# A second wait in a unit's gathers: the seventh gather of a unit waits for the rows of its second to sixth

## The chip, the cores and the metric

The kernel runs on one core of one Trainium2 chip. The metric is the device time of one execution in microseconds (us). The kernel before takes 5981.97 us, the median of three runs (5981.73 to 5982.89).

## What is computed

A graph network with 12,500 nodes of 64 features and 200,000 edges, the edges sorted by their destination. Two graph attention layers with four heads, then one layer with an attention over edges for each feature:

```python
def _gat(x, src, dst, W, att_src, att_dst, bias, n):
    xw = (x @ W).reshape(n, H, D)
    a_src = jnp.einsum('nhc,hc->nh', xw, att_src)
    a_dst = jnp.einsum('nhc,hc->nh', xw, att_dst)
    logits = jax.nn.leaky_relu(a_src[src] + a_dst[dst], NEG_SLOPE)
    m = jax.ops.segment_max(logits, dst, num_segments=n)
    ex = jnp.exp(logits - m[dst])
    s = jax.ops.segment_sum(ex, dst, num_segments=n)
    alpha = ex / (s[dst] + EPS)
    out = jax.ops.segment_sum(xw[src] * alpha[..., None], dst, num_segments=n)
    return out.mean(axis=1) + bias
...
h   = relu(_gat(x, ..., W1, ...) + (x @ lW1 + lb1))
y   = _gat(h, ..., W2, ...) + (h @ lW2 + lb2)
x   = layernorm(x + y)
# last layer, for each edge: relu([x[src], x[dst]] @ W_lin.T + b_lin), softmax over the edges of a
# destination, weighted sum of [x[src], x[dst]], @ W_out.T + b_out
x   = layernorm(x + last(x))
```

## The kernel before

**Units and passes.** The 200,000 edges are cut into units of 1,536 edges, twelve chunks of 128. There are 131 units; the last has only three chunks. The kernel makes three passes over all units: p = 0 and p = 1 are the two attention layers (the attention passes), p = 2 is the last layer. In each pass the rows of the source nodes are gathered from a table in HBM into SBUF. A row of the attention passes is 72 floats (288 bytes) wide, 128 rows a gather; a row of the last pass is 128 floats. When a pass is over, the rows that it stored are the table of the next pass.

**The gathers.** GpSimd (POOL) does nothing in the passes but issue gathers: one indirect DMA for each chunk, twelve a unit, one after the other (line 1075). So there are 130 x 12 + 3 = 1,563 in a pass and 4,689 in all. They fill `rows`, a ring of RING = 6 units. Before a unit's first gather POOL waits until the unit's indices are staged (`idx_staged`) and until the sums of the unit that used this place of the ring are done (`sums_ready >= n - RING + 2` in the attention passes), and it adds one to `go`, a counter that nobody waits for. The first gather of a unit counts on a semaphore of its own, `first_in`, the other eleven on `rows_in`, 16 for each gather. The first three units of pass 0 gather raw rows of x before the table is made, the fourth unit waits for the table.

**Who uses the rows.** In the attention passes ACT's `strip_of` (lines 1700, 1704, 1707) waits until all twelve gathers of a unit have landed, copies their attention terms, then waits for the first gather of the next unit (`first_in`) and copies that. From the strip PE makes the transposes of `fronts`, DVE the running maxima (lines 1327, 1332), PE adds them up (2067), DVE makes the logits (1345 to 1357), ACT the exponential (1746), DVE the shares (1392), and PE the sums over the rows themselves (`sums_of`, line 2085), which raise `sums_ready`. ACT copies the sums (`keep_sums`, line 1752), and PE, DVE and ACT make the output row of the unit, which SP stores (line 987). In the last pass DVE reads the rows itself (lines 1569, 1577, 1590, 1641).

**Other transfers.** ACT's queue fetches `rel_t` for a unit ahead (line 854, 336 KB), SP's queue fetches `own` (967) and `cut` (956) and stores the rows (987). Each engine runs its own hand-written order of these steps; they meet in semaphores alone. The order of POOL and the one user of the rows that waits for them in the attention passes stand below.

Of the kernel before, what the change touches and what calls it, by code (L numbers as in the profile page):

```python
# [50 lines left out]
def build(nc, x, src, dst, W1, att_src1, att_dst1, b1, lW1, lb1, W2, att_src2, att_dst2, b2, lW2, lb2,  # L51
# [9 lines left out]
    G = 12  # L61
# [47 lines left out]
    def landed(p, c, each, tail, each3=None, tail3=None):  # L109


        before = p * (each * len(range(c.s, NU, RING)) - (each - tail if (NU - 1) % RING == c.s else 0))
        if p == 2 and each3 is not None:
            each, tail = each3, tail3
        return 16 * each * c.q + 16 * (before + (tail if c.at_least(NU - 1) else each))
# [5 lines left out]
    def rest_landed(p, c):  # L121

        return landed(p, c, G - 1, LASTC - 1, G - 2, LASTC - 2)

    def chunks(c):
        return LASTC if c.at_least(NU - 1) else G
# [6 lines left out]
    with ctx:  # L133
# [20 lines left out]
        def sem(name):  # L154
            return ctx.enter_context(nc.semaphore(name))
# [259 lines left out]
        rows_in = [sem(f"rows_in{s}") for s in range(RING)]  # L415
# [86 lines left out]
        go = sem("go")  # L502
# [35 lines left out]
        def units(eng, end=NU):  # L538
            for u in range(RING):
                yield Unit(u // RING, u % RING)  # L540
            with eng.Fori(1, (NU - RING) // RING) as q:
                for s in range(RING):
                    yield Unit(q, s)
            for u in range((NU - RING) // RING * RING, end):
                yield Unit(u // RING, u % RING)
# [498 lines left out]
        @block.gpsimd  # L1044
        def _(pool):
            nc.gpsimd.memset(ident[:, :], 0.0).then_inc(consts_ready, 1)
            nc.gpsimd.memset(ones[:, :], 1.0).then_inc(consts_ready, 1)
            nc.gpsimd.iota(col_i[:, :], [[1, W]], base=0, channel_multiplier=0).then_inc(consts_ready, 1)
            nc.gpsimd.iota(row_i[:, :], [[1, 1]], base=0, channel_multiplier=1).then_inc(consts_ready, 1)
            pool.wait_ge(consts_ready, 4)  # L1050
            nc.gpsimd.affine_select(out=ident[:, :], in_=ident[:, :], compare_op=ALU.not_equal, fill=1.0,
                                    base=0, pattern=[[-1, P]], channel_multiplier=1)\
                .then_inc(consts_ready, 1)
            nc.gpsimd.memset(rows_g[:, 0:G * RAW, D:D + 1], 1.0).then_inc(consts_ready, 1)
            pool.wait_ge(consts_ready, 6)

            for p in range(3):
                if p > 0:
                    pool.wait_ge(row_stored, 32 * NU * p)
                for c in units(pool):  # L1060
                    n = NU * p + c.u
                    raw = p == 0 and c.below(RAW)
                    pool.wait_ge(idx_staged, RAW if raw else n + 1)
                    if p == 0 and c.below(RAW + 1) and c.at_least(RAW):
                        for k in range(len(XLOADED)):
                            pool.wait_ge(x_moved[k], XSTORED[k])
                            pool.sem_inc(go, 1)
                    if not c.below(RING):
                        if p < 2:
                            pool.wait_ge(sums_ready, n - RING + 2)  # L1070
                        else:
                            pool.wait_ge(share_ready, 4 * (n - RING + 1))
                    pool.sem_inc(go, 1)
                    for j in range(chunks(c)):
                        nc.gpsimd.indirect_dma_start(rows_of[p][:, G * c.s + j, 0:D] if raw else rows_of[p][:, G * c.s + j, :],  # L1075
                                                     None, x if raw else halves[p],
                                                     bass.IndirectOffsetOnAxis(ap=idx_now[:, c.s, j:j + 1], axis=0))\
                            .then_inc(first_in[c.s] if j < (2 if p == 2 else 1) else rows_in[c.s], 16)
            pool.wait_ge(end_ready, 1)
            for k, u in enumerate((FULL - 1, FULL)):  # L1080
                n = 2 * NU + u
                pool.wait_ge(row_kept_v, n + 1)
                if k == 0:
                    pool.wait_ge(row_stored, 32 * n)
                else:
                    pool.wait_ge(tail_stored, 16)
                nc.gpsimd.indirect_dma_start(out, bass.IndirectOffsetOnAxis(ap=end_at[0:W, k:k + 1], axis=0),
                                             row_out[u % 2][:, :], None, bounds_check=N - 1, oob_is_err=False)\
                    .then_inc(tail_stored, 16)
            pool.wait_ge(row_stored, 32 * (NU * 3 - 2))  # L1090
            pool.wait_ge(tail_stored, 32)
            pool.wait_ge(flag_ready, 1)
            with pool.If(pool.value_load(flag[0:1, 0:1], min_val=0, max_val=1) > 0):
                general[1](pool)

        @block.vector
        def _(dve):
# [224 lines left out]
            def segment_most(p, n, c, parts):  # L1322


                dve.wait_ge(cut_in[c.k], cuts_loaded(p, c))
                for cuts, values, running, _ in parts:
                    done = nc.vector.tensor_tensor_scan(running, cuts[:, 0:-1], values, NEG, ALU.add, ALU.max)  # L1327
                done.then_inc(upto_ready, 1)
                dve.wait_ge(upto_ready, n + 1)
                for cuts, _, running, to in parts:  # L1330
                    span = running.shape[1]
                    done = nc.vector.tensor_tensor_scan(to[:, span - 1:HALO - 1:-1], cuts[:, span:HALO:-1],  # L1332
                                                        running[:, span - 1:HALO - 1:-1], NEG, ALU.add, ALU.max)
                done.then_inc(most_ready, 1)
# [908 lines left out]
```

## Time and profile before

| | |
|---|---|
| time, median of 3 runs | 5981.97 us |
| span of the profiled execution | 8154.7 us |
| instructions in it | 86920 |
| PE busy | 4073.2 us, 50% |
| DVE busy | 3734.1 us, 46% |
| ACT busy | 2927.8 us, 36% |
| POOL busy | 4442.8 us, 54% |
| DMA, mean over the span | 55 GB/s |

The profiled execution is far longer than an ordinary one, and no time of it other than its span is given. So a stretch of the profile can't be taken for a stretch of an ordinary execution unless one knows what the extra 2,173 us consist of. POOL's times are those of single gathers; "idle before" is the time since the end of the gather before, with what ended it behind the arrow. An idle time put down to "issue" is one in which the engine waited for nothing that the profile shows, "remote" is a semaphore whose last increment the profile doesn't show.

### The profile page before, as it was taken

Reading aid. Unit: us, or ns where it says so; the run is one execution under the profiler, and the core shown is the slowest. Engines: PE = TensorE matmul, PEld = TensorE weight load, DVE = VectorE, ACT = ScalarE, POOL = GpSimd, SP = SyncE. Lnnn points to the kernel's source line nnn. Section 1 sums busy time; section 2 is a strip of 40 time slices with the busy share of each in tenths; the row PEclk is TensorE's granted clock in tenths of the full one; section 3 lists DMA queues with packets and bytes.
Section 4 is the critical chain, followed back from the end, with each engine's and each line's share of the span. In section 5 each row is a group of like instructions: output and inputs, shape, how many; then the busy total and the mean of one; then the engine's idle time right before and its main releaser. Section 6 shows DMA issues by size and latency. Waiting matters only on the chain. (4 is left out here: it accounts for less than half of the span.)

```text
span 8154.7 us, 86920 instructions
## 1 busy us (share of the span) xinstructions
PE 4073.2 (50%) x21983; PEld 3747.4 (46%) x21983; DVE 3734.1 (46%) x9512; ACT 2927.8 (36%) x5694; POOL 4442.8 (54%) x4701
## 2 busy tenths in 40 slices
PE   4445445444553555555555553445544444455455
PEld 4444444444442444444444443444444444444445
DVE  3333333333343444444444443555555555555556
ACT  2222222222222444444444442334333333344344
POOL 4666666666655666666666645444444444444442
PEclk6555555555565555555555565555555555555555
DMA  5222222222212222222222221111111111111111
GB/s 117 56 51 54 52 51 53 52 51 52 53 46 48 55 54 54 56 55 54 54 56 55 54 55 52 56 54 54 56 54 54 53 53 53 53 53 55 54 54 37
DMA packets 354021, 444.78 MB, mean 55 GB/s; under 512 B 142024, under 2 KB 233574, under 8 KB 353360
## 3 DMA queue, kind: packets, MB, share of 16 engines
q0 software_dynamic: 150112, 217.86, 13.4%
q10 hardware_dynamic: 50400, 132.89, 4.7%
q1 hardware_dynamic: 153424, 93.06, 4.4%
q8 instruction: 35, 0.57, 0.0%
q14 instruction: 50, 0.41, 0.0%
HBM read 407.90 MB, written 39.55 MB: 55 GB/s over the span
## 5 line engine op out<-in xcount | busy, mean ns | idle before, releaser
L1075 POOL DMA_INDIRECT rows<-tab,idx_now x4653 | 4404.9, 947 | 3600.9 <-issue 1586.1
L2197 PE MATMUL psum<-hot,prob 128*128 128x112 f32 x3126 | 776.5, 406 | 889.3 <-issue 879.4
L2085 PE MATMUL psum<-share,rows 128*65 128x132 f32 (+10 forms) x6240 | 1175.4, 380 | 0.1
L2197 PEld LDWEIGHTS psum<-hot,prob 128*128 128x128 f32 x3126 | 708.3, 316 | 933.1 <-issue 928.1
L2085 PEld LDWEIGHTS psum<-share,rows 128*65 128x65 f32 x6240 | 1092.0, 223 | 5.8 <-DVE share L1392 0.2
L1382 DVE TENSOR_SCALAR share_prev<-psum,prev_all 128x4 f32<-128x4 f32 x258 | 57.2, 222 | 2262.8 <-remote 2255.0
L2181 PE MATMUL psum<-own,hot_t 112*128 112x64 f32 x3126 | 687.2, 416 | 763.6 <-DVE mix L1548 585.1
L2181 PEld LDWEIGHTS psum<-own,hot_t 112*128 112x128 f32 x3126 | 664.3, 325 | 795.5 <-issue 580.8
L1752 ACT ACTIVATE sums<-psum 65x448 f32<-65x448 f32 x260 | 140.6, 541 | 2068.1 <-remote 2053.4
L1590 DVE TENSOR_TENSOR near<-psum,rows 128x768 f32<-128x768 f32 x131 | 124.9, 953 | 1424.2 <-remote 1386.6
L1720 ACT ACTIVATE std<-mean_var,eps 112x1 f32<-112x1 f32 x262 | 77.7, 297 | 1868.4 <-DVE mean_var L1420 1756.1
L2112 PE MATMUL psum<-w_next,turned 65*112 65x72 f32 x262 | 83.6, 422 | 1084.6 <-ACT turned L1756 1084.5
L1685 ACT ACTIVATE hot_t<-away,ones 112x1536 bf16<-112x1536 f32 (+2 forms) x393 | 616.9, 1570 | 12.8
L1683 ACT ACTIVATE away<-rel_t,minus_row 112x1536 f32<-112x1536 bf16 (+1 forms) x393 | 612.9, 1560 | 13.0 <-DMA rel_t<-rel_runs 6.7
L2112 PEld LDWEIGHTS psum<-w_next,turned 65*112 65x112 f32 x262 | 58.1, 282 | 1118.7 <-ACT turned L1756 943.0
L1392 DVE TENSOR_TENSOR share<-hot,psum 128x400 f32<-128x400 f32 (+2 forms) x780 | 487.5, 681 | 2.0 <-issue 1.4
L1327 DVE TENSOR_TENSOR_SCAN psum<-cut,psum 48x224 f32<-48x224 bf16 (+3 forms) x524 | 448.3, 878 | 81.4 <-PE psum L2058 49.9
L2097 PE MATMUL psum<-w_heads,sums 65*112 65x65 f32 x2080 | 441.8, 390 | 1.5 <-DVE mix L1412 1.1
L2097 PEld LDWEIGHTS psum<-w_heads,sums 65*112 65x112 f32 x2080 | 414.0, 303 | 2.2 <-ACT sums L1752 2.1
L2115 PE MATMUL psum<-w_edge,turned 65*112 65x192 f32 x262 | 126.7, 586 | 560.4 <-ACT turned L1756 560.4
L1332 DVE TENSOR_TENSOR_SCAN most<-cut,psum 48x176 f32<-48x176 bf16 (+3 forms) x524 | 394.6, 774 | 13.9 <-DVE psum L1327 0.3
L1746 ACT ACTIVATE psum<-logit 128x48 f32<-128x48 f32 (+1 forms) x262 | 56.4, 215 | 955.0 <-issue 877.7
(246 smaller groups left out, 6228.3 us busy)
## 6 DMA issues: line engine op xcount, KB each, us to landing
rel_t<-rel_row ACTq DMA_DIRECT2D x256, 336.0 KB
rows<-tab,idx_now POOLq DMA_INDIRECT x4653
rel_t<-rel_runs ACTq DMA_DIRECT2D x128, 336.0 KB
own<-tab SPq DMA_DIRECT2D x262, 63.0 KB
cut<-cut_row SPq DMA_DIRECT2D x130, 120.2 KB
tab<-row SPq DMA_DIRECT2D x131, 112.0 KB
tab<-row SPq DMA_DIRECT2D x131, 63.0 KB
own<-tab SPq DMA_DIRECT2D x131, 56.0 KB
```

Of the source, the lines that this page charges most:

```text
L1075: nc.gpsimd.indirect_dma_start(rows_of[p][:, G * c.s + j, 0:D] if raw else rows_of[p][:, G * c.s + j, :], None, x if raw else halves[p], b ...
L1327: done = nc.vector.tensor_tensor_scan(running, cuts[:, 0:-1], values, NEG, ALU.add, ALU.max)
L1332: done = nc.vector.tensor_tensor_scan(to[:, span - 1:HALO - 1:-1], cuts[:, span:HALO:-1], running[:, span - 1:HALO - 1:-1], NEG, ALU.add, ...
L1392: nc.vector.tensor_tensor(to[:, j0:j1, :, 0:w], hot[c.k][:, j0:j1, 0:w].unsqueeze(2).to_broadcast([P, j1 - j0, H, w]), prob[c.k][:, j0:j1, ...
L1683: nc.scalar.activation(away[:, 0:e], rel_t[k][:, 0:e], ACT.Abs, bias=minus_row[0:W, 0:1]).then_inc(away_ready, 1)
L1685: nc.scalar.activation((hot_b if p < 2 else hot_t)[k][:, 0:e], away[:, 0:e], ACT.Relu, bias=ones[0:W, 0:1], scale=-1.0)\
L1752: nc.scalar.activation(sums_kept_in(c)[:, :, 0:w], summed[:, :, 0:w], ACT.Copy).then_inc(sums_kept, 1)
L2085: done = nc.tensor.matmul(summed[:, :, LO[j]:HI[j]], rows_g[:, at + j, 0:D + 1], of[:, j, :, 0:SUBS[j]], start=not opened, stop=j == chunk ...
L2097: done = nc.tensor.matmul(mixed_of(c)[:, h, :], sums_kept_in(c)[:, h, :], w_heads[p][:, h, :], start=True, stop=True)
L2112: nc.tensor.matmul(extra[:, 0:2 * H + D], turned[:, 0:W], w_next[:, :], start=True, stop=True)\
L2181: done = nc.tensor.matmul(added3[:, j, :], hot_t[k][:, P * j:P * j + P], own3[c.s][:, 0:D], start=True, stop=True)
L2197: done = nc.tensor.matmul(summed3, prob3[k][:, j, :], hot3[k][:, j, :], start=not opened, stop=j == chunks(c) - 1, skip_group_check=True)
```

## The change

Three lines are put into POOL's loop over the twelve gathers of a unit. In the attention passes POOL waits ahead of gather j = 6, the seventh, until `rows_in` of the unit's place has reached `rest_landed(p, c)` less 96. `rest_landed` is the count when all eleven gathers of the unit that raise `rows_in` have landed, so this is the count when five of them have: j = 1 to 5, the second to the sixth. Then it adds one to `go`. The last unit of a pass has three gathers and so no such wait. The third pass is as before.

```diff
@@ -1072,6 +1072,9 @@
                             pool.wait_ge(share_ready, 4 * (n - RING + 1))
                     pool.sem_inc(go, 1)
                     for j in range(chunks(c)):
+                        if p < 2 and j == G // 2:
+                            pool.wait_ge(rows_in[c.s], rest_landed(p, c) - 16 * (G // 2))
+                            pool.sem_inc(go, 1)
                         nc.gpsimd.indirect_dma_start(rows_of[p][:, G * c.s + j, 0:D] if raw else rows_of[p][:, G * c.s + j, :],
                                                      None, x if raw else halves[p],
                                                      bass.IndirectOffsetOnAxis(ap=idx_now[:, c.s, j:j + 1], axis=0))\
```

## Rows read from the trace of the kernel before

**Rows 1.** Groups by line, POOL: us 500 to 2400 (pass 0), us 5000 to 7800 (last pass)

```profile
L1075 POOL DMA_INDIRECT rows<-tab,idx_now x1264 | 1195.4, 946 | 706.9 <-issue 493.5 <-remote 213.4
...
L1075 POOL DMA_INDIRECT rows<-tab,idx_now x1351 | 1278.5, 946 | 1523.3 <-ACT idx_now L1673 1129.6 <-issue 393.7
```

**Rows 2.** Timeline of POOL at the start: first, twelfth, thirteenth gather (start, duration)

```profile
4.40 1.12 POOL L1075 DMA_INDIRECT rows<-in_x,idx_now  x1 [2.41 <-DVE idx_now L1105]
...
18.37 0.95 POOL L1075 DMA_INDIRECT rows<-in_x,idx_now  x1 [0.31 <-issue]
19.62 0.95 POOL L1075 DMA_INDIRECT rows<-in_x,idx_now  x1 [0.30 <-issue]
```

**Rows 3.** Timeline of all engines, one unit in the middle of pass 0

```profile
1402.29 0.54 ACT L1752 ACTIVATE sums<-psum 65x448 f32<-65x448 f32 x1 [10.11 <-remote]
...
1403.07 0.95 POOL L1075 DMA_INDIRECT rows<-tab,idx_now  x1 [3.33 <-remote]
1403.11 0.20 ACT L1707 ACTIVATE strip<-rows 128x4 f32<-128x4 f32 x1
...
1404.95 0.32 ACTq L854 DMA_DIRECT2D rel_t<-rel_row  x1
...
1407.09 4.70 PE L2085 MATMUL psum<-share,rows 128*65 128x52 f32 x24
```

**Rows 4.** Timeline of ACT and POOL, third and fourth unit of pass 0

```profile
166.23 0.54 ACT L1752 ACTIVATE sums<-psum 65x448 f32<-65x448 f32 x1 [2.57 <-PE psum L2085]
...
175.77 0.54 ACT L1752 ACTIVATE sums<-psum 65x448 f32<-65x448 f32 x1 [2.08 <-PE psum L2085]
...
176.55 0.95 POOL L1075 DMA_INDIRECT rows<-tab,idx_now  x1 [32.00 <-PE psum L2085]
```

**Rows 5.** Timeline of PE and DVE in the last pass

```profile
6012.47 0.35 PE L2197 MATMUL psum<-hot,prob 128*128 128x112 f32 x1 [2.54 <-issue]
...
6026.67 0.96 DVE L1590 TENSOR_TENSOR near<-psum,rows 128x768 f32<-128x768 f32 x1 [21.50 <-remote]
...
6041.17 0.96 DVE L1590 TENSOR_TENSOR near<-psum,rows 128x768 f32<-128x768 f32 x1 [0.61 <-PE psum L2204]
```

**Rows 6.** Waits of POOL over the whole span: us, times, longest

```profile
POOL rows L1075 <- DMA tab<-row: 96.9, 2, 52.3
POOL out L1087 <- DVE row_out L1426: 88.2, 2, 84.8
```

**Rows 7.** Timeline of POOL, first gather from the table in pass 0

```profile
97.41 0.94 POOL L1075 DMA_INDIRECT rows<-tab,idx_now  x1 [47.56 <-DMA tab<-x_tab]
```

**Rows 8.** Timeline of POOL and ACT at the start of pass 1

```profile
2475.28 0.94 POOL L1075 DMA_INDIRECT rows<-tab,idx_now  x1 [0.30 <-issue]
...
2476.53 0.95 POOL L1075 DMA_INDIRECT rows<-tab,idx_now  x1 [0.31 <-issue]
...
2477.85 0.25 ACT L1704 ACTIVATE strip<-rows 128x48 f32<-128x48 f32 x1 [7.21 <-DMA rows<-tab,idx_now]
...
2478.95 0.21 ACT L1707 ACTIVATE strip<-rows 128x4 f32<-128x4 f32 x1 [0.84 <-DMA rows<-tab,idx_now]
```

**Rows 9.** Timeline of SP's queue and POOL at the end of pass 0

```profile
2460.50 0.33 SPq L854 DMA_DIRECT2D rel_t<-rel_row  x1
...
2461.32 0.94 POOL L1075 DMA_INDIRECT rows<-tab,idx_now  x1 [44.55 <-DMA tab<-row]
```

**Rows 10.** Timeline of POOL and DVE at the start of the last pass

```profile
4873.30 0.95 POOL L1075 DMA_INDIRECT rows<-tab,idx_now  x1 [0.30 <-issue]
...
4880.52 0.31 DVE L1569 STREAM_TRANSPOSE outer<-rows 128x128 f32<-128x128 f32 x1 [10.35 <-DMA rows<-tab,idx_now]
```

**Rows 11.** The page's DMA queues: packets, MB, share of 16 engines' span

```profile
q0 software_dynamic: 150112, 217.86, 13.4%
q10 hardware_dynamic: 50400, 132.89, 4.7%
```

**Rows 12.** Groups by line, POOL, whole span

```profile
L1075 POOL DMA_INDIRECT rows<-tab,idx_now x4653 | 4404.9, 947 | 3600.9 <-issue 1586.1 <-ACT idx_now L1673 1248.4 <-remote 568.1
```

## The prediction

> **What bounds the kernel now.** The profiled execution took 8154.7 us of span and the runs have a median of 5981.97 us, so the first question is which of the profile's times an ordinary execution has too. I read the groups by line for POOL first. A gather is 0.95 us of work, in every pass [rows 1]. In pass 0 there are 1264 gathers in 1900 us, or 18.04 us for a unit of twelve; in the last pass 1351 in 2800 us, 24.87 us for a unit. Next the timeline of POOL where nothing holds it, at the start: the first gather starts at 4.40, the twelfth at 18.37 and the thirteenth, which belongs to the next unit and has a wait and an increment of `go` ahead of it, at 19.62 [rows 2]. So the pace is 1.25 us from start to start (0.95 of work and 0.30 between), a unit takes 12 x 1.25 = 15.0 us, and a wait that is already met costs nothing that shows.
>
> Then the timeline of a unit in mid-pass. POOL waits 3.3 us at the unit's first gather, and ACT has waited 10.1 us for the same thing, the sums of a unit [rows 3]. It looks as if the compute engines bound the passes. But in this unit PE's sums start at 1407.09 and are through 4.70 us later, 9.5 us after ACT's start at 1402.29 [rows 3], and where nothing is late ACT's next start follows them: 9.54 us for a unit (166.23 to 175.77) [rows 4]; in the last pass it takes 14.50 us (6026.67 to 6041.17), after a stretch in which PE's matmuls came one by one, 2.5 us apart, for nothing that the trace shows, and DVE waited 21.5 us [rows 5]. The late semaphores are PE's slow stretches, and I take them for the cost of being profiled. Without them compute needs 9.5 us a unit in the attention passes and 14.5 in the last, both less than POOL's 15.0.
>
> The median bears this out. 4,689 gathers x 1.25 = 5861 us. The start adds 4.4 [rows 2] and 47.3 for the table (47.56 less the usual 0.30) [rows 7], which makes 5913. On top come POOL's wait for the ring in pass 0, 32.0 [rows 4], the two turns between passes, 96.9, and the end, 84.8 [rows 6]: all of them would make 6127. These last four are too long in the profile, because there POOL is up to six units ahead when its gathers end, and would be one or two units ahead otherwise. 5982 lies between 5913 and 6127. So in an ordinary execution POOL issues gathers back to back through all three passes, and that sets the time.
>
> **The change, part by part.** It removes nothing and moves no transfer past another. It adds a wait and an increment of `go` ahead of the seventh gather of each of the 130 full units of passes 0 and 1, 260 in all. Behind the wait on POOL stand the unit's six other gathers and every later unit; for them wait ACT's `strip_of` and all compute behind it. SP's and ACT's own transfers have no part in the wait.
>
> What the sixth gather needs to land: of the gather that starts at 2475.28, ACT uses the rows at 2477.85, 2.57 us after its start; of the next, started at 2476.53, at 2478.95, 2.42 us [rows 8]. In both cases ACT was idle and waiting, so its start shows the landing. I take 2.50.
>
> What POOL needs to go on: at 175.77 ACT starts on the sums of unit 1, and POOL, idle for 32 us and waiting for the same increment, starts its gather at 176.55, 0.78 later [rows 4]. In mid-pass it is 0.78 again (1402.29 to 1403.07) [rows 3]. After a transfer, where SP and POOL both wait for the last store of the pass, SP issues at 2460.50 and POOL starts at 2461.32, 0.82 later [rows 9]. The instructions after the wait are the same there as here: an increment of `go`, then a gather. I take 0.78.
>
> So the seventh gather starts 2.50 + 0.78 = 3.28 us after the sixth instead of 1.25: 2.03 us more for a unit, 17.03 in place of 15.0. The wait is not in the cover of anything, since compute is done with its 9.54 us and waits for rows. A unit's compute just starts 2.03 us later.
>
> Where it is covered: the first three units of pass 0 are gathered before the 47.56 us wait for the table [rows 7], and the next three before the 32.0 us wait for the ring [rows 4]; 3 x 2.03 = 6.1 us goes under in each. If that cover is thinner, the six units cost up to 12 us. That leaves 254 units x 2.03 = 516 us. The turns between passes and the end stay as they are: the seventh gather's delay is over before the last gather of a pass. 5982 + 516 = **6498 us**, forecast 6500.
>
> The Trainium skill, "DMA: Bandwidth & Descriptors", "Anatomy of one DMA — SWDGE (gpsimd) path", gives a GpSimd DMA about 2.0 us fixed and bytes / 436e3 on top, so an estimated 2.08 us for 36.9 KB. Counted from the gather's start that is shorter than the 2.42 to 2.57 of [rows 8] and would make 1.61 us a unit and 6391 us; counted from the end of its 0.95 us of work it would make 2.56 us a unit and 6632 us. The rows lie between the two readings.
>
> **Bounds of the unknown.** The wait in mid-unit itself has no row. Least: POOL goes on as fast as ACT does after a landing; then 2.50 - 1.25 = 1.25 us a unit, 5982 + 318 = 6300. Most: the sixth gather lands late because other transfers are in its way. ACT's queue fetches `rel_t` 1.84 us after the strip's last copy (1403.11 to 1404.95) [rows 3]. In an ordinary execution that copy comes 2.42 us after the unit's first gather, so the fetch starts near 4.3, and the sixth gather at 6.25. The packets of one such fetch take 4.7% x 8154.7 / 387 = 1.0 us of all 16 DMA engines, those of one gather 13.4% x 8154.7 / 4689 = 0.23 us [rows 11]. If the whole fetch ran ahead of the sixth gather each time, the unit would lose 3.03 us: 5982 + 770 = 6750. A gather at the crowded start of the last pass needed 7.22 us (4873.30 to 4880.52) [rows 10], but there the table's, the edges' and the cuts' first loads of a pass are all out at once; I hold that for a few units at the start at most, some 10 us in all. Since the fetch is mostly over when the sixth gather's packets run, the value is nearest to the undisturbed 2.50.
>
> **The rivals.**
>
> *The landing is late in every unit* (3.03 us, 6750). For it: the timing above puts the fetch just ahead of the sixth gather. Against it: one microsecond of packets has two to be gone in. The Trainium skill, same page, "Queues, rings and completion order", says that each DMA engine takes turns between its queues packet by packet; by that a gather is delayed by at most what the other queue has left, and no run before shows a gather beside just one fetch.
>
> *POOL goes on sooner* (1.25 to 1.6 us, 6300 to 6390). For it: profiling may lengthen both terms. Against it: 0.78 to 0.82 three times.
>
> *The wait is swallowed* (not slower, 5982). The mechanism is the wait for `sums_ready` at the unit's first gather. If compute and not POOL bounded the attention passes, POOL would have slack there and the wait in mid-unit would only move it: 12 x 1.25 + 2.03 = 17.03 us against the profile's own 18.04 us [rows 1, 3]. It decides from a compute cycle of 17.03 us on. Against it: 9.54 us undisturbed [rows 4], and a cycle of 17 in two passes and 15 in the last would make 131 x 49 = 6419 us before, not 5982.
>
> *It gets faster*: only by shorter gathers, if spacing them kept the descriptor queue from filling. The 4,653 gathers from the tables take 4404.9 us, 0.947 each, where single ones in mid-pass take 0.94 to 0.95 [rows 12]: less than 15 us in all is there to be won.
>
> **How the numbers follow.** Forecast (2.0 to 2.2 us a unit, 6480 to 6545, with differences of profiled and ordinary runs 6400 to 6660): 0.78. Late landing, above 6660: 0.08. Sooner, below 6400: 0.07. Swallowed: 0.05. Faster: 0.02. A range of 6390 to 6670 leaves out somewhat less than 2 in 10. A measurement tells 0.2% (12 us) from nothing, and every case but the last two is far beyond it: slower 0.93, same 0.05, faster 0.02.
>
> **What the changed profile would show.** The sum is made for an ordinary execution. In the profiled one the wait is the rival's case: 17.03 is below 18.04, so its span should stay near 8155 us (within 1%), the first gather's idle time in mid-pass should shrink from 3.3 to about 1.3, and the seventh's should be 0.30 + 2.03 = 2.3 instead of 0.30, released by the gather's DMA. The seventh gather should start 3.3 us after the sixth. The last pass should be as it was. If the median rises by about 516 us while the span of the profile stays, the reading of the two kinds of execution was right. It is wrong if the seventh's idle time differs from 2.3, or if the median stays where it is, since POOL then didn't bound the attention passes.

## The result and the profile after

The changed kernel takes 6621.09 us, the median of four runs (6612.66 to 6623.88), against 5981.85 us for the kernel before (four runs, 5981.19 to 5982.89). The ratio is 1.1069, 95% interval 1.1056 to 1.1082: slower by 639 us. The forecast was 6500 us with a range of 6390 to 6670.

One thing has to be said before any number below can be read. The kernel before is not equally fast on all chips: where the results above were measured it takes 5982 us, on the chip of the second set of experiments 5989, but on those of the first and the third set 8185 and 8086, profiled or not. The first profile of the kernel before, with its span of 8154.7, is of the second kind, and so it is compared with the runs on such chips only. I call the two kinds quick and slow chips, though each was met at one time only, so that it is the chip and nothing else of that time isn't shown.

The page of the changed kernel comes from a quick chip; its span is its run's time, 6621.49 us, less 2 us:

```profile
span 6619.7 us, 87256 instructions
...
PE 3930.2 (59%) x21983; PEld 3609.8 (55%) x21983; DVE 3695.7 (56%) x9512; ACT 2961.8 (45%) x5694; POOL 4437.0 (67%) x4701
...
L1078 POOL DMA_INDIRECT rows<-tab,idx_now x4653 | 4390.6, 944 | 2105.6 <-issue 1564.2
...
L2200 PE MATMUL psum<-hot,prob 128*128 128x112 f32 x3126 | 669.4, 408 | 10.9 <-DVE prob L1644 10.9
...
rows<-tab,idx_now POOLq DMA_INDIRECT x4653, 2.5
```

The last line is of the page's DMA issues: 2.5 us from a gather's issue to its landing, the median of 4,653. The gathers' own work is as before, 0.944 us each [rows 12]. The timeline of all engines in mid-pass 0: the sixth gather of a unit, the seventh and the eighth, and ACT and DVE at a unit's sums:

```profile
1409.07 0.94 POOL L1078 DMA_INDIRECT rows<-tab,idx_now  x1 [0.30 <-issue]
...
1412.33 0.94 POOL L1078 DMA_INDIRECT rows<-tab,idx_now  x1 [2.32 <-DMA rows<-tab,idx_now]
...
1413.43 0.54 ACT L1755 ACTIVATE sums<-psum 65x448 f32<-65x448 f32 x1 [1.44 <-PE psum L2088]
1413.54 0.22 DVE L1385 TENSOR_SCALAR share_prev<-psum,prev_all 128x4 f32<-128x4 f32 x1 [2.06 <-PE psum L2088]
...
1413.58 0.94 POOL L1078 DMA_INDIRECT rows<-tab,idx_now  x1 [0.30 <-issue]
```

The seventh starts 3.26 us after the sixth, having idled for 2.32 us until the gathers' DMA released it. ACT waits 1.4 us for the sums that it waited 10.1 us for in the first profile [rows 3]. What ACT waits long for is now the rows themselves, as `strip_of` shows in the same timeline:

```profile
1404.05 0.21 ACT L1703 ACTIVATE strip<-rows 128x4 f32<-128x4 f32 x1 [7.88 <-DMA rows<-tab,idx_now]
...
1405.33 0.21 ACT L1710 ACTIVATE strip<-rows 128x4 f32<-128x4 f32 x1 [0.93 <-DMA rows<-tab,idx_now]
```

The page has it for all units of both attention passes, 5.7 us of waiting for the gathers in each:

```profile
L1703 ACT ACTIVATE strip<-rows 128x4 f32<-128x4 f32 x260 | 53.3, 205 | 1476.8 <-DMA rows<-tab,idx_now 1476.7
```

So compute stands behind POOL. In the last pass POOL waits for nothing. The groups by line of POOL, us 5000 to 6500; the idle time is the 0.30 us between gathers and no more:

```profile
L1078 POOL DMA_INDIRECT rows<-tab,idx_now x1203 | 1135.2, 944 | 366.6 <-issue 366.6
```

Compare [rows 1]: there the same pass had 1130 us of waiting in 2800. Its 1,563 gathers now take from 4625.85 to 6575.83 us, 1.25 us each.

**Where the 639 us are.** I read the start of every gather from POOL's timeline. In pass 0 the seventh gathers start 3.95 us after the sixth in the mean, with a median of 3.41; in pass 1 3.63 and 3.29. Against the plain 1.25 us the 260 gaps add 351.5 + 308.7 = 660.2 us. The first three of pass 0 account for 23.1 of it. They come ahead of the first gather from the table, and if the wait for the table covers them, 637.1 us are exposed. The measured difference is 639.2.

Most gaps are the forecast's 3.28, but not all. Every fourth unit, the same units in both passes (u = 13, 17, ... 129, and u = 9 as well in pass 1), has a gap of about 4.6 in pass 0 and 4.5 in pass 1. One pair of gathers of such a unit, from the timeline:

```profile
1042.06 0.94 POOL L1078 DMA_INDIRECT rows<-tab,idx_now  x1 [0.30 <-issue]
...
1046.81 0.94 POOL L1078 DMA_INDIRECT rows<-tab,idx_now  x1 [3.81 <-issue]
```

Sorted by u modulo 4, the medians are 3.39, 4.63, 3.40 and 3.38 in pass 0 and 3.27, 4.52, 3.27 and 3.27 in pass 1.

**Which part of the gap is longer.** The trace also holds each increment of `rows_in` by a gather that lands. So a gap can be cut in two at the last increment that the wait asked for: what the sixth gather needs to land, and what POOL needs from there to the seventh. The medians from the eleventh unit on:

| units of the changed kernel | sixth gather's start to the last landing | last landing to the seventh's start |
|---|---|---|
| pass 0, u not 1 modulo 4 | 2.59 us | 0.80 us |
| pass 0, u = 1 modulo 4 | 2.60 us | 2.02 us |
| pass 1, u not 1 modulo 4 | 2.47 us | 0.80 us |
| pass 1, u = 1 modulo 4 | 2.49 us | 2.02 us |

The rows are not late in the outliers. POOL goes on late: 2.02 us after the landing in 61 units (30 in pass 0, 31 in pass 1), 0.79 to 0.81 us in the 199 others, with nothing in between. The row above says so too. Its idle time is put down to "issue", since no semaphore was raised just ahead of it, where a plain gap has "DMA". POOL's waits over the whole span:

```profile
POOL rows L1078 <- issue: 1574.0, 4487, 4.9
POOL rows L1078 <- DMA rows<-tab,idx_now: 490.7, 196, 10.8
```

The 61 late ones are what the second line lacks of the 257 waits for gathers from the table. Together they cost 61 x 1.22 = 75 us.

The landing is what is long at the crowded start of pass 0, where the sixth and seventh unit have gaps of 11.70 and 8.55 us, 10.91 and 7.75 of it until the landing. The DMA engines are busy for 67% of the first 165 us there, and for 25% from us 1000 to 1165:

```profile
133.16 0.94 POOL L1078 DMA_INDIRECT rows<-tab,idx_now  x1 [10.76 <-DMA rows<-tab,idx_now]
...
155.43 0.94 POOL L1078 DMA_INDIRECT rows<-tab,idx_now  x1 [7.60 <-DMA rows<-tab,idx_now]
```

### The profile page after: what moved, and what is told of

It is laid out like the page before. It is cut to its first block and busy times, and to the rows that moved or that the text cites. A ratio compares the mean times of both kernels' runs of the same rounds, so it can differ in the third digit from the quotient of the medians.

```text
span 6619.7 us, 87256 instructions
## 1 busy us (share of the span) xinstructions
PE 3930.2 (59%) x21983; PEld 3609.8 (55%) x21983; DVE 3695.7 (56%) x9512; ACT 2961.8 (45%) x5694; POOL 4437.0 (67%) x4701
## 5 line engine op out<-in xcount | busy, mean ns | idle before, releaser
L2061 PE MATMUL psum<-ident,strip 128*48 128x128 f32 (+1 forms) x786 | 210.3, 405 | 1703.8 <-ACT strip L1710 1703.5
L2061 PEld LDWEIGHTS psum<-ident,strip 128*48 128x48 f32 (+1 forms) x786 | 83.1, 133 | 1789.2 <-issue 1776.0
L2184 PE MATMUL psum<-own,hot_t 112*128 112x64 f32 x3126 | 654.9, 403 | 319.7 <-DVE mix L1551 300.5
L2184 PEld LDWEIGHTS psum<-own,hot_t 112*128 112x128 f32 x3126 | 633.1, 312 | 345.3 <-issue 238.3
L1703 ACT ACTIVATE strip<-rows 128x4 f32<-128x4 f32 x260 | 53.3, 205 | 1476.8 <-DMA rows<-tab,idx_now 1476.7
L2200 PE MATMUL psum<-hot,prob 128*128 128x112 f32 x3126 | 669.4, 408 | 10.9 <-DVE prob L1644 10.9
L2200 PEld LDWEIGHTS psum<-hot,prob 128*128 128x128 f32 x3126 | 649.8, 319 | 11.1 <-DVE prob L1644 11.1
L2106 PE MATMUL psum<-ident,row 112*64 112x112 f32 x262 | 80.7, 308 | 270.6 <-DVE row L1429 266.3
```

Source lines behind the costliest of these rows:

```text
L2184: done = nc.tensor.matmul(added3[:, j, :], hot_t[k][:, P * j:P * j + P], own3[c.s][:, 0:D], start=True, stop=True)
L2200: done = nc.tensor.matmul(summed3, prob3[k][:, j, :], hot3[k][:, j, :], start=not opened, stop=j == chunks(c) - 1, skip_group_check=True)
```

## The experiments

Theory A: POOL's issue of gathers sets the time of an ordinary execution; a wait costs what its releaser is late, 2.50 us for the landing and 0.78 for going on, less the 1.25 that the next gather would have taken anyway. Rivals: the wait or its increment costs something in itself; compute takes the delay up; and, for the surplus over 3.28, ACT's fetch of `rel_t` delays the landings. The expectations below take the gathers of every fourth unit for late, which the table above does not bear out.

**First set, a slow chip (before: 8184.53 us, median of 13 runs).**

*The kernel before, profiled again.* No edit.

> The kernel before, unchanged, for a second profile. The profile of before had a span of 8154.7 us against a median of 5982; the profile of the changed kernel has 6619.7 against 6621. Theory 1, that profiling slows PE in this kernel whenever the gathers run ahead of it: the span is again near 8155, with 3.3 us of idle time ahead of each unit's first gather in passes 0 and 1. Theory 2, that the first profile caught a peculiar execution: the span is within 1% of 5982, the gathers run at 1.25 us from start to start through all passes, and the waits ahead of first gathers are gone but for the turns between passes.

Measured 8188.28 us, and the span is 8186.4. The span and the waits are those of theory 1, but its reason is wrong. The median of thirteen runs of the kernel before is 8184.53 us on this chip, so it is no odd execution; and on the quick chip the changed kernel's profiled run took what its other runs took, so it is no cost of profiling. POOL's waits in it:

```profile
POOL rows L1075 <- issue: 1605.4, 4449, 3.7
POOL rows L1075 <- ACT idx_now L1673: 1261.6, 65, 20.6
POOL rows L1075 <- remote: 586.1, 169, 3.7
```

They are those of the first profile within 4% [rows 12].

*The wait asks for the first gather only.*

```diff
-                            pool.wait_ge(rows_in[c.s], rest_landed(p, c) - 16 * (G // 2))
+                            pool.wait_ge(first_in[c.s], first_landed(p, c))
```

> The wait stays ahead of the seventh gather of the 260 units but asks only for the unit's first gather, which started 7.5 us before and lands 2.5 us after its start. Theory POOL pace (the wait costs what its releaser is late, nothing in itself): 5982 us within 0.2%. Rival (the wait and the increment of go in mid-unit cost POOL something themselves, for instance 0.8 us each time for going on): 260 x 0.78 = +203, 6185 us.

Measured 8195.84 us, ratio 1.0017 (1.0007 to 1.0028): +11 us. Two seventh gathers near the start of pass 0 (u = 6 and 7) come 7.67 and 4.98 us after the sixth, since the first gather landed that late; they are 10 of the 11 us. But for three more units at the start of pass 0 or 1 (1.44 to 2.67 us) the gap is 1.25 to 1.29 in the rest of both passes. So a wait that is met at once adds nothing to the gap. POOL has slack on this chip, so the time alone would not have shown it; the gaps do.

*The third gather waits for the first.*

```diff
-                        if p < 2 and j == G // 2:
-                            pool.wait_ge(rows_in[c.s], rest_landed(p, c) - 16 * (G // 2))
+                        if p < 2 and j == 2:
+                            pool.wait_ge(first_in[c.s], first_landed(p, c))
```

> The wait stands ahead of the third gather and asks for the unit's first. The first lands 2.50 us after its start, POOL goes on 0.78 us later, so the third gather starts 3.28 us after the first instead of 2.50: +0.78 us a unit. Theory POOL pace with landing 2.50 and restart 0.78: 254 to 260 units x 0.78 = +198 to +203, 6180 to 6185 us. Rival (restart is as quick as ACT's): 5982 us. Rival (a wait costs a full round trip wherever it stands, as 2.46 us a unit did in the change): 6620 us. If other transfers made the change's landings late, the surplus over 6185 is small here, since ACT's fetch of rel_t starts only 4.4 us after the unit's first gather.

Measured 8245.96 us, ratio 1.0073 (1.0056 to 1.0089): +61 us. The gap from the second to the third gather has a median of 1.98 us in pass 0 and 1.97 in pass 1. The first gather starts 1.25 us ahead of the second, so the third starts 3.22 us after the first: the chain of landing and going on is 3.2 us here too, and 0.72 us of it are exposed in the unit (the forecast said 0.78). Of 260 x 0.72 = 187 us the time shows 61.

*The fourth gather waits for the second and third.*

```diff
-                        if p < 2 and j == G // 2:
-                            pool.wait_ge(rows_in[c.s], rest_landed(p, c) - 16 * (G // 2))
+                        if p < 2 and j == 3:
+                            pool.wait_ge(rows_in[c.s], rest_landed(p, c) - 16 * 9)
```

> The wait stands ahead of the fourth gather and asks for the second and third. The third starts 2.5 us into the unit and lands at 5.0; ACT's fetch of rel_t is issued 4.4 us into it, so its packets are still ahead. Theory collision (what the change cost over 3.28 us a gap comes from ACT's fetch running just ahead of the sixth gather): gaps of 3.28 without the outliers of 4.6, 254 to 260 x 2.03 = +516 to +528, 6498 to 6510 us. Rival (the surplus has nothing to do with the fetch, such as gathers landing late every fourth unit by themselves): the same as the change, 6621 us, with a gap of 4.6 in every fourth unit.

Measured 8365.53 us, ratio 1.0218 (1.0201 to 1.0235): +181 us. The median gap is 3.60 us in pass 0 and 3.25 in pass 1, but the units fall into two sorts on this chip: in pass 0 every other unit both waits some 4 us at its first gather and has a gap of 4.1 to 4.3. Neither number of the expectation is met, since both were worked out for a quick chip. Yet the run is evidence on the fetch. In the units with the long gap ACT issues the fetch 1.9 us into the unit, just ahead of the third gather, for which the wait asks:

```profile
1420.32 0.95 POOL L1078 DMA_INDIRECT rows<-tab,idx_now  x1 [2.91 <-remote]
...
1422.19 0.32 ACTq L854 DMA_DIRECT2D rel_t<-rel_row  x1
...
1422.82 0.94 POOL L1078 DMA_INDIRECT rows<-tab,idx_now  x1 [0.30 <-issue]
...
1426.76 0.94 POOL L1078 DMA_INDIRECT rows<-tab,idx_now  x1 [3.00 <-DMA rows<-tab,idx_now]
```

From the twelfth unit of pass 0 on, 56 units have a gap above 3.9 us, and each has the fetch at that place; their third gather lands 3.39 us after its start, and POOL goes on after 0.80. In the 58 units with a gap under 3.5 no fetch is issued. So the third gather lands 0.9 us late where a fetch is issued just ahead of it.

**Second set, a quick chip (before: 5988.75 us, median of 7 runs).**

*The tenth gather waits for the second to ninth.*

```diff
-                        if p < 2 and j == G // 2:
-                            pool.wait_ge(rows_in[c.s], rest_landed(p, c) - 16 * (G // 2))
+                        if p < 2 and j == 9:
+                            pool.wait_ge(rows_in[c.s], rest_landed(p, c) - 16 * 3)
```

> The wait stands ahead of the tenth gather and asks for the second to ninth. The ninth starts 10 us into the unit, well after ACT's fetch of rel_t (4.4 us) and after SP's store, own and cut transfers (6.8 to 9.1 us into it, or up to 2 us earlier). Theory collision with rel_t: gaps of 3.28 without outliers, 6498 to 6510 us. Rival (gathers land late every fourth unit by themselves): 6621 us. Rival (SP's transfers, which now lie just ahead, delay it): gaps above 3.28 in most units, up to 6650 us.

Measured 6518.5 us, ratio 1.0887 (1.0869 to 1.0905): +530 us. POOL's waits:

```profile
POOL rows L1078 <- issue: 1348.8, 4425, 0.3
POOL rows L1078 <- DMA rows<-tab,idx_now: 610.5, 257, 11.2
```

The gap has a median of 3.26 us in pass 0, 3.28 in pass 1, with no outlier in pass 1 (3.19 to 3.95) and those of the start alone in pass 0. This is theory A to the number: 3.28 us a gap. The gaps add 551.5 us, 19.7 of them ahead of the first gather from the table: 531.8 exposed, 529.75 measured. The same wait three gathers later is 109 us cheaper than the change. What is missing are the outliers of every fourth unit, some of the late landings at the start, and the 0.13 us by which pass 0's median was above pass 1's. POOL goes on 0.80 us after the landing in all 260 units here, u = 1 modulo 4 among them.

*One address for the fetch, in the changed kernel.*

```diff
-            eng.dma_start(rel_t[c.k][:, 0:e], (rel_row if p < 2 else rel_runs)[bass.ds(UE * c.u, e)].partition_broadcast(W))\
+            eng.dma_start(rel_t[c.k][:, 0:e], (rel_row[0:e] if p < 2 else rel_runs[bass.ds(UE * c.u, e)]).partition_broadcast(W))\
```

> The change, and in the attention passes every fetch of rel_t reads the same 3 KB of HBM, unit 0's; leaves out: the destinations' places of the other units. In the change the seventh gather comes 4.6 instead of 3.3 us after the sixth in every fourth unit, the same units in both passes (9, 13, 17, ...). Theory address (the fetch of a unit whose 3,072 bytes lie badly in HBM takes longer, and 4 x 3,072 is a multiple of 4,096): the outliers are gone or stand in all units; gone makes 6621 less 2 x 30 x 1.25 = 6546 us. Rival (the period of four comes from elsewhere, from a queue or from time): 6621 us, outliers as they are.

Measured 6620.89 us, ratio 1.1055 (1.1037 to 1.1074). The outliers stand in the same units, 4.61 and 4.52 us in the median. The address is not their cause, and POOL's 2.02 us after the landing is as it was.

*A short fetch, in the changed kernel.* ACT's fetches write 16 of 112 partitions.

```diff
-            eng.dma_start(rel_t[c.k][:, 0:e], (rel_row if p < 2 else rel_runs)[bass.ds(UE * c.u, e)].partition_broadcast(W))\
+            eng.dma_start(rel_t[c.k][0:(W if eng is nc.sync or p == 2 else 16), 0:e], (rel_row if p < 2 else rel_runs)[bass.ds(UE * c.u, e)].partition_broadcast(W if eng is nc.sync or p == 2 else 16))\
```

> The change, and in the attention passes ACT's fetches of rel_t write 16 of the 112 partitions (48 KB instead of 336 KB); leaves out: the other 96 partitions, which keep older values. Theory collision (the fetch's packets make the sixth gather late): all gaps near 3.28, 254 to 260 x 2.03, 6498 to 6510 us. Rival (the surplus isn't the fetch's): 6621 us with the outliers of 4.6 in every fourth unit.

Measured 6614.18 us, ratio 1.1045 (1.1027 to 1.1064). A seventh of the fetch's bytes saves 7 us, and the gap of u = 57 in pass 0 is there as before, 4.68 us:

```profile
1039.61 0.95 POOL L1078 DMA_INDIRECT rows<-tab,idx_now  x1 [0.30 <-issue]
...
1044.29 0.94 POOL L1078 DMA_INDIRECT rows<-tab,idx_now  x1 [3.73 <-issue]
```

So ACT's fetch does not make the outliers. It does make gathers land late, but others than the one on which the seventh waits. In the changed kernel it is issued 4.3 us into the unit, as the prediction had it, 0.6 us after the fourth gather starts. From its own start the fourth gather then needs 3.67 us to land and the fifth 3.33, against 2.44 and 2.46 for the second and third. With the short fetch they need 2.82 and 2.45. By the time the sixth lands, that is over: 2.59 and 2.47 us in the two passes, 2.58 and 2.46 with the short fetch.

By the Trainium skill ("DMA: Bandwidth & Descriptors", "Queues, rings and completion order") each DMA engine takes turns between its queues packet by packet. The fourth gather's delay of 1.2 us is no less than the 1.0 us that the prediction reckons for all of the fetch's packets. So here the gather isn't seen to get through between them, and why not is open.

**Third set, a slow chip again (before: 8086.35 us, median of 11 runs).**

*The kernel before, profiled a third time.* No edit.

> The kernel before, unchanged, profiled once more. Two chips have given 8184 and 5989 us for it. If this chip runs it near 5985: the span is the time less 2 us, the gathers run at 1.25 us from start to start, no unit's first gather waits, and POOL's stops at the ring in pass 0, at the turns and at the end are those that the change's profile has (23.5, 29 and 29 us), not the 44.6, 52.3 and 84.8 of the first profile. If near 8185: the same 3.3 us at each unit's first gather as in the first profile.

Measured 8085.71 us; the span is 8083.9. It is the second case of the expectation. PE's matmuls of the last pass, a stretch of the timeline:

```profile
6003.05 0.34 PE L2197 MATMUL psum<-hot,prob 128*128 128x112 f32 x1 [1.34 <-issue]
...
6005.84 0.35 PE L2197 MATMUL psum<-hot,prob 128*128 128x112 f32 x1 [2.45 <-issue]
...
6008.64 0.35 PE L2197 MATMUL psum<-hot,prob 128*128 128x112 f32 x1 [2.45 <-issue]
```

and the same group in the groups by line, which have the matmuls at 407 ns each as on the quick chip (408), but 866 us of idle time before them where that one has 10.9:

```profile
L2197 PE MATMUL psum<-hot,prob 128*128 128x112 f32 x3126 | 776.6, 407 | 866.0 <-issue 857.6 <-DVE prob L1641 4.6
```

The matmuls are no longer; they start late. From us 5000 to 6500 the mean granted clock is 0.53 here and 0.58 on the quick chip, while PE is busy for 751 and 1147 us; matmuls of one length on both say that the clock isn't what holds them up.

*The wait asks for the first gather only, again.* The edit is that of the first set.

> The wait ahead of the seventh gather, for the unit's first gather alone, which landed about 5 us before. On the chip with 8185 us it made 0.17%. If this chip runs the kernel before near 5985, where POOL has no slack: by theory (the wait costs what its releaser is late and nothing in itself) within 0.2% of before; by the rival (the wait and the increment cost POOL 0.78 us themselves) +203 us.

Measured 8103.51 us, ratio 1.0029 (1.0015 to 1.0042): +17 us, near the 11 of the other slow chip. So no quick chip has timed this kernel. What the quick chip shows instead is the unit's first gather in the changed kernel, which also stands behind waits that are met and an increment of `go`: in pass 1 it starts 1.248 us after the gather before it, in the mean of 129.

*The fifth gather waits for the second to fourth.*

```diff
-                        if p < 2 and j == G // 2:
-                            pool.wait_ge(rows_in[c.s], rest_landed(p, c) - 16 * (G // 2))
+                        if p < 2 and j == 4:
+                            pool.wait_ge(rows_in[c.s], rest_landed(p, c) - 16 * 8)
```

> The wait stands ahead of the fifth gather, for the second to fourth. If the chip runs the kernel before near 5985: with plain gaps of 3.28 it is +528 us (260 units), with the outliers of 4.5 in every fourth unit +610 to +640 as in the change. It tells which gather lands late every fourth unit: outliers here, it is one of the first four; none, it is the fifth or sixth (or no gather but what runs beside it 6 to 9 us into the unit). On a chip with 8185 us: about +181 us, as with the wait at the fourth.

Measured 8144.13 us, ratio 1.0072 (1.0055 to 1.0089): +58 us, a third of what was expected. The gap's medians are 3.26 and 3.25, and by u modulo 4 they don't differ (3.23 to 3.27). POOL's waits show where the 2 us a unit went: the 169 "remote" waits of the first gathers, 541 us in the kernel before, are 90 and 239 us. Over both passes the gaps grow by 568 us, and what stands ahead of the units' first gathers shrinks by 513. That leaves 55 of the 58.

```profile
POOL rows L1078 <- DMA rows<-tab,idx_now: 384.7, 151, 11.5
POOL rows L1078 <- remote: 239.2, 90, 3.1
```

*Two waits in a unit,* that of the change and that of the tenth gather.

```diff
                         if p < 2 and j == 6:
                             pool.wait_ge(rows_in[c.s], rest_landed(p, c) - 16 * 6)
                             pool.sem_inc(go, 1)
+                        if p < 2 and j == 9:
+                            pool.wait_ge(rows_in[c.s], rest_landed(p, c) - 16 * 3)
+                            pool.sem_inc(go, 1)
```

> Two waits in each of the 260 units, the change's ahead of the seventh gather and that of the run with the tenth. If POOL's own pace sets the time, the two add up: +637 and +530 us, some +1165 us, 7150 us, at a cycle of 19.3 us in the attention passes. Rival (compute bounds a cycle of some 17 us and takes part of it): clearly less than the sum. On a chip with 8185 us, where compute holds POOL up 3.3 us a unit, two waits of 2.03 are 1.0 us a unit more than that slack: +270 us or more.

Measured 8392.84 us, ratio 1.0378 (1.036 to 1.0395): +306 us, as expected for a slow chip. Two gaps of 3.26 and 3.21 us in one unit, and a first gather that waits for nothing any more, from the timeline:

```profile
1171.07 0.94 POOL L1081 DMA_INDIRECT rows<-tab,idx_now  x1 [2.32 <-DMA rows<-tab,idx_now]
...
1176.78 0.94 POOL L1081 DMA_INDIRECT rows<-tab,idx_now  x1 [2.27 <-DMA rows<-tab,idx_now]
...
1180.52 0.94 POOL L1081 DMA_INDIRECT rows<-tab,idx_now  x1 [0.30 <-issue]
```

The unit's cycle has a median of 19.05 us, 12 x 1.25 + 2 x 2.03, where the kernel before has 17.83 on this chip: with two waits POOL sets the pace of the attention passes even on a slow chip, with one at the fifth gather (18.07 and 18.64) it barely does. And the outliers are back in the gap ahead of the seventh gather, 4.47 and 4.49 us in the median, in the units with u = 1 modulo 4 as on the quick chips, and again with 2.03 us from the landing to POOL's start. The gap ahead of the tenth in the same units has 3.24, with 0.80.

## Why the prediction was right, and where it was not

**That POOL bounds an ordinary execution at 1.25 us a gather: right.** The changed kernel's last pass, untouched by the change, has 1,563 gathers at 1.25 us without one wait, and its attention passes have ACT waiting for rows. The argument was made from the median and not from the profile's waits, and that was what saved it. The terms of its sum beside the gathers are those of a slow chip all the same. In the changed kernel the two turns are 50.7 us in place of 96.9, POOL's wait at the end 29.1 in place of 84.8, and the fourth unit's first gather waits for no table: it starts 80.88 us into the span, 0.30 after the end of the gather before it, where the first profile has 97.41 and a wait of 47.56 [rows 7]. So the sum's 5913 and 6127 are too high for a quick chip, if anything. The conclusion doesn't hang on them, since the gathers' 5861 are 98% of 5982.

**What the first profile's waits are: wrong.** I put PE's slow stretches down to profiling. They are no cost of profiling: the kernel before takes 8086 to 8185 us on such chips in every run. So the forecast for the profile after failed as well, "its span should stay near 8155 us": it is 6619.7, since the profile is from a quick chip. Why PE's matmuls come late on the slow ones is open; no run tells it.

**The price of one wait, 2.50 + 0.78 - 1.25 = 2.03 us: right.** The gap of 3.28 is 3.29 in pass 1, 3.26 and 3.28 with the wait at the tenth gather. The forecast idle time of 2.3 us is 2.32. Both terms hold by themselves: the landing takes 2.47 to 2.59 us, POOL's going on 0.80. But the second holds for 199 of the 260 waits only. The first gather's idle time, forecast at 1.3 us for a profile like the first, is 0.30, since the profile is from a quick chip. By the Trainium skill's fit ("DMA: Bandwidth & Descriptors", "Anatomy of one DMA — SWDGE (gpsimd) path") such a gather takes an estimated 2.08 us. That is below the 2.5 us that the profile's page gives from issue to landing, and the 6391 us worked out from it were 230 us low. The other reading, counted from the end of the gather's work, gave 6632, near the result but for a wrong reason: it makes a gap of 3.81 us, and the plain gaps are 3.26 to 3.41.

**The number of waits exposed and the surplus: too small, 516 for 639 us.** The term that was too small is "254 units x 2.03". In its place stand 257 units. That the wait for the table covers the first three is borne out only by the sum, which balances within 2 us with their 23 us of gaps left out. The 32 us wait for the ring, on which the next three were to be hidden, belongs to the slow chip, and no first gather waits there in the changed kernel. The 257 plain waits are 522 us. POOL's late going on in 61 units is 75 us and was not foreseen at all. The sixth and seventh unit of pass 0 with their 11.70 and 8.55 us are 14 us over the plain gap, where the text allowed 10 us for the crowded start. Pass 0's higher gap, from a sixth gather that lands 0.12 us later than in pass 1, is 0.13 x 130 = 17 us. That is 628 of 637.

**The rival of a late landing: rightly held improbable.** It had the fetch of `rel_t` in the sixth gather's way. The fetch delays the fourth gather by 1.2 us and the fifth by 0.9, and has passed when the sixth lands, as the prediction argued. With the wait at the fourth gather on a slow chip the collision is there, 0.9 us. The surplus over the forecast has another cause: with a seventh of the fetch's bytes it stays, with one address too, and it lies behind the landing.

**The rival that the wait is swallowed: wrong where the result was measured, and largely right on a slow chip.** Its threshold was the compute cycle: 17.03 us of POOL's against 18.04. With the wait at the fifth gather 58 us of some 520 are left, with the third gather's wait 61 of 187; with two waits, 19.06 us, POOL passes the cycle and the time rises by 306. The changed kernel itself was not timed on a slow chip.

**Open.** Why POOL goes on 2.02 us after the landing, and not 0.80, in every fourth unit. What is known: the rows have landed in time; it is in the same units in both passes, in the changed kernel and in three variants, on a quick and on a slow chip; it moves with the units and not with the time (69.8 us apart in pass 0 and 69.4 in pass 1 of the changed kernel, 77.3 with two waits); it is at the seventh gather and not at the tenth of the same unit; and it isn't the fetch's size or address. The profile shows nothing that POOL does in that 1.2 us, and no run shifted POOL's instructions while it left the wait where it is. Open is also why PE's matmuls come late on some chips.

## What to carry to other kernels

An engine that issues back to back and bounds the kernel pays a wait for its own transfer in full: the landing, plus its own restart, less one issue; here 2.03 us for a plain wait, 199 of 260, and nothing at all where the rows asked for had long landed. Where a wait is longer than that, cut it in two at the landing before you look for who is in the transfer's way: here two runs changed the transfer, and it was the engine that went on late. Before a profile's waits are taken for the kernel's, hold the span beside the timed median: where they differ by a third, the count of instructions of the suspected bound times their pace, against the median, is the better witness. And where a second bound is near, a wait's price is no property of the kernel alone: one at the fifth gather cost 58 us on a chip that holds compute up, where one at the seventh and one at the tenth cost 639 and 530 on chips that don't.

## What the runs showed of the hardware that was not expected

- The same program took 5982 and 5989 us in two sets of runs and 8185 and 8086 in two others, with the same 407 ns for a matmul and 866 us instead of 10.9 of idle time before one group of 3,126 of them.
- POOL goes on 0.80 us after the last landing that its wait asks for, and 0.78 us after ACT does on the same increment.
- In 61 of 260 units, always with u = 1 modulo 4, POOL went on 2.02 us after that landing, in the changed kernel and in three variants, on a quick and on a slow chip.
- A fetch of 336 KB issued 0.6 us after a gather's start made that gather land 1.2 us late, 3.67 in place of 2.45 us; one of 48 KB, 0.4 us.
- At the start of pass 0, with the DMA engines busy for 67% of the time, the gap at a wait was up to 11.7 us in the changed kernel (16.5 with two waits in a unit), in place of 3.3.
